# Half-size load buffers, doubled stage buffers and bf16 transposes in an eight-core attention-plus-masked-FFN kernel

## The reference

```python
xn = _layernorm(x, axis=-1)                       # x: (8, 2048, 2048), f32
# attention branch, 16 heads of 128, no softmax
q = relu(xn @ Wq) / SCALE; k = relu(xn @ Wk) / SCALE; v = xn @ Wv; u = silu(xn @ Wu)   # per head
kv = einsum('bhlk,bhlv->bhkv', k, v)
out = srms_norm(einsum('bhlk,bhkv->bhlv', q, kv)) * u
s = out @ Wo
# FFN branch: a router keeps 4 of 16 blocks for each token
mask = one_hot(top_k(softmax(xn @ Wr.T + br), 4))
h = gelu(einsum('nf,ibf->nib', xn, W1b)) * mask[:, :, None]     # W1b: 16 blocks of 512
g = silu(einsum('nib,fib->nf', h, W2b))
return x + s * g
```

## Time and profile before

| | |
|---|---|
| median of 2 runs | 6756.02 us (6677.65 to 6834.38) |
| the profiled execution | 6742.81 us, span 6741.0 us on core 3, the slowest |
| spans of the 8 cores | 6653.4 to 6741.0 us, mean granted TensorE clock 0.80 to 0.81 |
| busy share of the span | PE 54%, weight loads 22%, VectorE 19%, ScalarE 15%, GpSimd 6% |
| the chain that ended last | PE 50%, DMA 18%, VectorE 12%, ScalarE 9%, issue 8% |
| first transpose L209, last | 20.8 us, 657.0 us (stage 0) |
| first K matmul L308, last | 707.4 us, 1414.1 us (stage 1) |
| first W1 matmul L407, last W2 matmul L439 | 1428.1 us, 4487.3 us (stage 3) |
| first q matmul L510, last `bcp` matmul L564 | 4547.9 us, 6091.6 us (stage 2) |
| first output matmul L612, last | 6133.9 us, 6721.0 us (stage 4) |

### The profile page before, as it was taken

How to read it: one execution, slowest core, us unless ns; L and a number is a source line. 1 busy time by engine, 2 the same in 40 slices (tenths; PEclk the granted TensorE clock), 3 DMA queues, 4 the chain that set the end, 5 groups by cost and what they waited for, 6 DMA issues and landing times.

```text
span 6741.0 us, 45880 instructions; the slowest of 8 cores (6653.4 to 6741.0 us)
## 1 busy us (share of the span) xinstructions
PE 3666.1 (54%) x14994; PEld 1507.5 (22%) x14994; DVE 1300.4 (19%) x1958; ACT 985.9 (15%) x1317; POOL 378.5 (6%) x556
## 2 busy tenths in 40 slices
PE   2222777676666667656666766734444444444444
PEld 1111222232222223222222322311111111111111
DVE  2332000001222111112211111112223222321000
ACT  1111111111111111121111111111111111110000
POOL 0000000000000000000000000000000000002222
PEclk9999877898888888878888888866666666667777
DMA  1000111112222332322233232220000000003333
GB/s 39 25 26 22 47 50 50 44 59 86 89 89 90 94 100 81 100 75 88 88 94 100 81 100 83 86 81 13 25 25 19 19 25 25 13 25 78 93 90 89
DMA packets 130040, 422.73 MB, mean 63 GB/s; under 512 B 17104, under 2 KB 17104, under 8 KB 127760
## 3 DMA queue, kind: packets, MB, share of 16 engines
q1 hardware_dynamic: 83968, 251.76, 12.1%
q0 software_dynamic: 45840, 168.03, 8.3%
...
## 4 chain that ended last, share of the span: by engine, by line
PE 50%; DMA 18%; DVE 12%; ACT 9%; issue 8%; POOL 2%; DVEq 1%; ACTq 0%; POOLq 0%; SPq 0%
PE hps L407 15%; PE yps L439 14%; DMA w2ring<-w2t 7%; DMA gst<-gscr 4%; PE kp L308 4%; PE qp L510 4%; PE vp L313 4%; PE qp L519 3%; DVE srow L559 3%; ACT w1b L398 2%; ACT hm L411 2%; PE bcp L564 2%; PE pt L209 2%; DMA woring<-wo 2%; DVE w2b L428 2%
## 5 line engine op out<-in xcount | busy, mean ns | idle before, releaser
L439 PE MATMUL yps<-w2b,hm 128*128 128x512 bf16 x4096 | 946.4, 396 | 710.3 <-DVE w2b L428 710.3
L407 PE MATMUL hps<-A,w1b 128*128 128x512 bf16 x4096 | 1007.9, 409 | 317.0 <-ACT w1b L398 317.0
L439 PEld LDWEIGHTS yps<-w2b,hm 128*128 128x128 bf16 x4096 | 412.1, 101 | 1244.6 <-issue 802.0
L407 PEld LDWEIGHTS hps<-A,w1b 128*128 128x128 bf16 x4096 | 416.9, 104 | 908.8 <-issue 515.4
L612 PE MATMUL sps<-wob,osb 128*128 128x512 bf16 x1024 | 286.5, 445 | 342.2 <-ACT wob L598 198.6
L510 PE MATMUL qp<-A,wqb 128*128 128x512 bf16 x1024 | 255.2, 416 | 305.2 <-ACT wub L499 305.2
L447 DVE TENSOR_TENSOR y_acc<-y_acc,yps 128x1024 f32<-128x1024 f32 x224 | 273.6, 1222 | 597.5 <-PE yps L439 597.5
L564 PE MATMUL bcp<-srow,onesrfs 1*128 1x512 f32 x128 | 130.6, 1121 | 429.2 <-DVE srow L559 429.2
L308 PE MATMUL kp<-wkb,A 128*128 128x512 bf16 x1024 | 270.8, 425 | 146.0 <-ACT wvb L295 146.0
L415 DVE TENSOR_TENSOR hm<-hm,mbc 128x1024 bf16<-128x1024 bf16 x128 | 88.6, 692 | 1334.8 <-ACT hm L411 1334.8
L426 POOL DMA_DIRECT2D w2ring<-w2t x128 | 68.5, 535 | 3755.0 <-DVE w2b L428 3742.7
...
## 6 DMA issues: line engine op xcount, KB each, us to landing
w1ring<-w1r SPq DMA_DIRECT2D x256, 512.0 KB, 4.8
w2ring<-w2t SPq DMA_DIRECT2D x128, 512.0 KB, 5.4
w2ring<-w2t POOLq DMA_DIRECT2D x128, 512.0 KB, 4.4
...
wring<-wqr POOLq DMA_DIRECT2D x32, 512.0 KB, 4.8
wring<-wur POOLq DMA_DIRECT2D x32, 512.0 KB, 4.4
```

Source lines behind the costliest of these rows:

```text
L407: p.e("tensor", lambda e, i=i, ii=ii, ng=ng, sl=sl, hf=hf, tok0=tok0: e.matmul(hps[sl][:, ng * 512:(ng + 1) * 512], w1b[hf][:, ii * 128:(i ...
L439: p.e("tensor", lambda e, t8=t8, jc=jc, fg=fg, sl=sl: e.matmul(yps[sl][:, fg * 512:(fg + 1) * 512], hm[:, jc * 1024 + t8 * 128: jc * 1024 ...
```

## The change

Only the parts that the prediction speaks of; `...` marks what is left out. In stage 0 the split into high and low parts is made before the transposes, on the whole tile, and both parts are transposed as bf16. In stage 3 `w2b` gets two buffers (one for each fh), the W2 pieces are halved and cast by ScalarE, the mask rows come in halves through one buffer, and the silus work in place and are written out as f32. In stage 2 the body is split into `stage_qu(h)` and `stage_attn(h)`, called one head apart, with two buffers for `qtsb`, `utsb` and `attnsb`, half-size load pieces, and the squares done in two halves. In stage 4 `gst` is f32.

```diff
-    g_d = nc.dram_tensor("gscr", [L, D], BF16, kind="Internal").ap()
+    g_d = nc.dram_tensor("gscr", [L, D], F32, kind="Internal").ap()
...
+        xn_done = p.v(cV)
+        p.w("scalar", cV, xn_done)
+        p.e("scalar", lambda e: e.copy(out=xnhi[:], in_=xn32[:]), inc=cS)
+        hi_done = p.v(cS)
+        p.w("vector", cS, hi_done)
+        p.e("vector", lambda e: e.tensor_tensor(out=xnlo[:], in0=xn32[:], in1=xnhi[:], op=OP.subtract), inc=cV)
         ln_done[t] = p.v(cV)
...
-            p.e("tensor", lambda e, t=t, c=c, slot=slot: e.transpose(slot[:, 0:128], xn32[:, c * 128:(c + 1) * 128], idn32[:]), inc=cT)
+            p.e("tensor", lambda e, t=t, c=c, slot=slot: e.transpose(slot[:, 0:128], xnhi[:, c * 128:(c + 1) * 128], idnbf[:]))
+            p.e("tensor", lambda e, t=t, c=c, lslot=ptl[c % 2]: e.transpose(lslot[:, 0:128], xnlo[:, c * 128:(c + 1) * 128], idnbf[:]), inc=cT)
...
-            p.w("vector", cS, ahi_done[t][c])
             if c >= 2:
                 p.w("vector", cT, rt_done_c[c - 2])
-            p.e("vector", lambda e, t=t, c=c, slot=slot: e.tensor_tensor(out=alo[c % 2][:], in0=slot[:, 0:128], in1=A[:, c * L + t * 128: c * L + (t + 1) * 128], op=OP.subtract), inc=cV)
+            p.w("vector", cT, tr_done[t][c])
+            p.e("vector", lambda e, t=t, c=c, lslot=ptl[c % 2]: e.tensor_copy(alo[c % 2][:], lslot[:, 0:128]), inc=cV)
...
-    w2b = p3.enter_context(nc.sbuf_tensor("w2b", [128, 8 * 1024], BF16))
+    w2b = [p3.enter_context(nc.sbuf_tensor(f"w2b{i}", [128, 8 * 1024], BF16)) for i in range(2)]
-    w2ring = [p3.enter_context(nc.sbuf_tensor(f"w2ring{i}", [128, 1024], F32)) for i in range(2)]
+    w2ring = [p3.enter_context(nc.sbuf_tensor(f"w2ring{i}", [128, 512], F32)) for i in range(2)]
-    mrow = [p3.enter_context(nc.sbuf_tensor(f"mrow{i}", [1, 1024], BF16)) for i in range(2)]
+    mrow = p3.enter_context(nc.sbuf_tensor("mrow0", [1, 512], BF16))
...
                 for gg in range(2):
-                    p.e("tensor", lambda e, bb=bb, gg=gg: e.matmul(hps[0][:, gg * 512:(gg + 1) * 512], onesrb[0:1, :], mrow[bb][0:1, gg * 512:(gg + 1) * 512], start=True, stop=True), inc=(cT if gg == 1 else None))
+                    p.w("sync", cS, mask_done[NT - 1])
+                    p.w("sync", cT, mrow_guard[0])
+                    mrow_dma = p.dma("sync", lambda e, b=b, gg=gg, tok0=tok0: e.dma_start(out=mrow[0:1, :], in_=maskT[b:b + 1, tok0 + gg * 512: tok0 + (gg + 1) * 512]), dS)
+                    p.wd("tensor", mrow_dma)
+                    p.e("tensor", lambda e, gg=gg: e.matmul(hps[0][:, gg * 512:(gg + 1) * 512], onesrb[0:1, :], mrow[0:1, :], start=True, stop=True), inc=cT)
+                    mrow_guard[0] = p.v(cT)
...
-                    p.w(qeng, cV, w2cast_slot[sl])
-                    dd = p.dma(qeng, lambda e, jg=jg, fh=fh, sl=sl: e.dma_start(out=w2ring[sl][:], in_=w2t_d[jg * 128:(jg + 1) * 128, fh * 1024:(fh + 1) * 1024]), qsem)
-                    p.wd("vector", dd)
-                    p.e("vector", lambda e, jc=jc, sl=sl: e.tensor_copy(w2b[:, jc * 1024:(jc + 1) * 1024], w2ring[sl][:]), inc=cV)
-                    w2cast_slot[sl] = p.v(cV)
+                    for cc in range(2):
+                        p.w(qeng, cS, w2cast_slot[cc])
+                        dd = p.dma(qeng, lambda e, jg=jg, fh=fh, cc=cc: e.dma_start(out=w2ring[cc][:], in_=w2t_d[jg * 128:(jg + 1) * 128, fh * 1024 + cc * 512: fh * 1024 + (cc + 1) * 512]), qsem)
+                        p.wd("scalar", dd)
+                        if jc == 0 and cc == 0:
+                            p.w("scalar", cT, w2cons_fh[fh])
+                        p.e("scalar", lambda e, jc=jc, fh=fh, cc=cc: e.copy(out=w2b[fh][:, jc * 1024 + cc * 512: jc * 1024 + (cc + 1) * 512], in_=w2ring[cc][:]), inc=cS)
+                        w2cast_slot[cc] = p.v(cS)
...
-            p.wd("scalar", gst_dma[0])
-            p.e("scalar", lambda e, t8=t8: e.activation(out=gstage[:], in_=y_acc[:, t8 * D:(t8 + 1) * D], func=AF.Silu), inc=cS)
+            p.e("scalar", lambda e, t8=t8: e.activation(out=y_acc[:, t8 * D:(t8 + 1) * D], in_=y_acc[:, t8 * D:(t8 + 1) * D], func=AF.Silu), inc=cS)
...
-            for hf in range(2):
-                sslot = (h * 4 + (0 if wdst is wqb else 2) + hf) % 2
+            for hf in range(4):
+                sslot = hf % 2
...
-        qu_done = p.v(cS)
-        p.w("tensor", cS, qu_done)
+        qu_done[h] = p.v(cS)
+
+    def stage_attn(h):
+        par = h % 2
+        p.w("tensor", cS, qu_done[h])
...
-        p.e("vector", lambda e: e.tensor_tensor(out=sq32[:], in0=attnsb[:], in1=attnsb[:], op=OP.mult), inc=cV)
...
+        for hh2 in range(2):
+          p.e("vector", lambda e, par=par, hh2=hh2: e.tensor_tensor(out=sq32[:], in0=attnsb[par][:, hh2 * 1024:(hh2 + 1) * 1024], in1=attnsb[par][:, hh2 * 1024:(hh2 + 1) * 1024], op=OP.mult), inc=cV)
...
+    for h in range(NH):
+        stage_qu(h)
+        if h >= 1:
+            stage_attn(h - 1)
+    stage_attn(NH - 1)
...
-    gst = [p4.enter_context(nc.sbuf_tensor(f"gst{i}", [128, 512], BF16)) for i in range(2)]
+    gst = [p4.enter_context(nc.sbuf_tensor(f"gst{i}", [128, 512], F32)) for i in range(2)]
```

More of the change, by code:

```diff
@@ L138, in build @@
     nc.const_aps.register(F32, INV_SCALE, cst[:, 1:2])
-    for dst, src in ((idn32, idn32_d), (idnbf, idnbf_d), (onescol, onescol_d),
-                     (onesrb, onesrb_d), (onesrf, onesrf_d), (wrt32, wrr_d),
+    for dst, src in ((idnbf, idnbf_d), (onescol, onescol_d),
+                     (onesrb, onesrb_d), (onesrf, onesrf_d),
                      (br1, br_d), (cst, cst_d)):
         p.dma("gpsimd", lambda e, dst=dst, src=src: e.dma_start(out=dst[:], in_=src[:]), dG)
+    p0 = ExitStack()
+    wrt32 = p0.enter_context(nc.sbuf_tensor("wrt32", [128, NC * NB], F32))
+    p.dma("gpsimd", lambda e: e.dma_start(out=wrt32[:], in_=wrr_d[:]), dG)
     p.dbar("vector", dG)
@@ L163, in build @@
     maskb = p0.enter_context(nc.sbuf_tensor("maskb", [128, NB], BF16))
-    pt = [p0.enter_context(nc.psum_tensor(f"pt{i}", [128, 512], F32)) for i in range(2)]
+    pt = [p0.enter_context(nc.psum_tensor(f"pt{i}", [128, 128], BF16)) for i in range(2)]
+    ptl = [p0.enter_context(nc.psum_tensor(f"ptl{i}", [128, 128], BF16)) for i in range(2)]
     plog = p0.enter_context(nc.psum_tensor("plog", [128, 512], F32))
@@ L433, in build @@
+                w2_ready = p.v(cS)
+                p.w("tensor", cV, hm_ready)
+                p.w("tensor", cS, w2_ready)
                 for t8 in range(8):
                     sl = t8 % 2
-                    if t8 >= 2:
-                        p.w("tensor", cV, yadd[t8 - 2])
+                    p.w("tensor", cV, yadd_slot[sl])
                     for jc in range(8):
                         for fg in range(2):
-                            p.e("tensor", lambda e, t8=t8, jc=jc, fg=fg, sl=sl: e.matmul(yps[sl][:, fg * 512:(fg + 1) * 512], hm[:, jc * 1024 + t8 * 128: jc * 1024 + (t8 + 1) * 128], w2b[:, jc * 1024 + fg * 512: jc * 1024 + (fg + 1) * 512], start=(jc == 0), stop=(jc == 7)), inc=(cT if (jc == 7 and fg == 1) else None))
+                            p.e("tensor", lambda e, t8=t8, jc=jc, fg=fg, fh=fh, sl=sl: e.matmul(yps[sl][:, fg * 512:(fg + 1) * 512], hm[:, jc * 1024 + t8 * 128: jc * 1024 + (t8 + 1) * 128], w2b[fh][:, jc * 1024 + fg * 512: jc * 1024 + (fg + 1) * 512], start=(jc == 0), stop=(jc == 7)), inc=(cT if (jc == 7 and fg == 1) else None))
@@ L484, in build, with stage_qu @@
     o_done = {}
+    qu_done = {}
     wring2_slot = [0, 0]
-    for h in range(NH):
+    def stage_qu(h):
         par = h % 2
@@ L498, in build @@
                 first_cast = False
-                p.e("scalar", lambda e, par=par, hf=hf, sslot=sslot, wdst=wdst: e.copy(out=wdst[par][:, hf * 1024:(hf + 1) * 1024], in_=wring2[sslot][:]), inc=cS)
+                p.e("scalar", lambda e, par=par, hf=hf, sslot=sslot, wdst=wdst: e.copy(out=wdst[par][:, hf * 512:(hf + 1) * 512], in_=wring2[sslot][:]), inc=cS)
                 wring2_slot[sslot] = p.v(cS)
@@ L537, in build @@
             attn_evac[ng] = p.v(cV)
-        p.e("vector", lambda e: e.tensor_tensor(out=sq32[:], in0=attnsb[:], in1=attnsb[:], op=OP.mult), inc=cV)
-        sq_done = p.v(cV)
-        p.w("scalar", cV, sq_done)
-        p.e("scalar", lambda e: e.copy(out=sqh[:], in_=sq32[:]), inc=cS)
-        sqh_done = p.v(cS)
-        p.w("vector", cS, sqh_done)
-        p.e("vector", lambda e: e.tensor_tensor(out=sql[:], in0=sq32[:], in1=sqh[:], op=OP.subtract), inc=cV)
-        sql_done = p.v(cV)
-        p.w("tensor", cV, sql_done)
@@ L547, in build @@
-        for ng in range(4):
+        for hh2 in range(2):
+          p.e("vector", lambda e, par=par, hh2=hh2: e.tensor_tensor(out=sq32[:], in0=attnsb[par][:, hh2 * 1024:(hh2 + 1) * 1024], in1=attnsb[par][:, hh2 * 1024:(hh2 + 1) * 1024], op=OP.mult), inc=cV)
+          sq_done = p.v(cV)
+          p.w("scalar", cV, sq_done)
+          p.e("scalar", lambda e: e.copy(out=sqh[:], in_=sq32[:]), inc=cS)
```

(11 more changed lines are left out.)

81 lines of the change are left out of this document (39 added, 42 removed).

## The result

The changed kernel is slower: 1.032 times the time before (95% interval 1.022 to 1.042). The medians of all executions are 7032 us against 6876. Its profiled execution took 6831.29 us, span 6829.0 on core 6. The prediction said 6822 us and "within 2%", so the one number that it hit, the profiled time, hides that its start was wrong.

The account below looks back on a forecast made before the run. No single engine bounds the kernel; each stage is a chain of hand-overs between engines. Stage 0 -82, stage 3 +82, silus -36, stage 2 +89 and stage 4 +26 sum to +79 on 6742.8: 6822 us, range 6670 to 6935.

Parts of the forecast that it names:

- the gain of a chunk of stage 0: Stage 0, transposes and copies: each chunk saves 0.60 us (0.42 to 0.65), 256 chunks 154 us.
- the g piece: Stage 4, load of g doubled to 256 KB: 0.4 us more a tile, +26 us (0 to +45).
- from the last W2 matmul to the first W1 matmul: Stage 3, mask rows through one buffer delay the W1 loads: +7.0 us per slab (5 to 10).
- before fh 0: Stage 3, TensorE's wait for W2 loads and casts behind the last gelu: +10.7 us per slab.
- before fh 1: Stage 3, W2 loads and casts while TensorE does fh 0; wait 9.0 instead of 21.0, -12.0 us per slab.
- the silus: Stage 3, silus in place need 2.0 us each instead of standing 5.55 apart: -36 us (-50 to -10).
- short landings: Rival, faster: 256 KB pieces land 0.7 us sooner in stage 3 and the head loads; 6598 us, chance 0.07.
- longer hand-overs: Rival, slower: stage 3 mask-row DMAs take 2.8 us, SP rounds 4.7; slab +10.5, 6908 us, chance 0.20.
- (a): Stage 2, eight 256 KB loads a head instead of four of 512 KB: +4.75 us for 15 heads, +69 in all.
- (b): Stage 2, squares in halves: +2.1 us each, 16 x 2.1 = +34 us.
- (c): Stage 2, `ap` matmuls no longer wait for the last evacuation of u: about -0.9 x 16 = -14 us.
- the skew overlaps nothing: Stage 2, engines run in order, so the norm chain still stands alone, with no q, u matmuls beside it.

## Why the prediction was wrong, and where it was right

**In short.** Every step of the forecast happened in the direction that it said, and its sum still came to +79 us where the typical core lost 144. The terms that failed are sizes: the gain of a chunk of stage 0 (0.60 us said, 0.50 measured), the price of small pieces in a head (4.75 said, 5.8 measured), the g piece (0.4 said, 0.5 measured) and the time around the steps of stage 3 (9 us more). They failed all in one direction, and together they pass the 2% within which the forecast stayed.

**The base.** The sum was made against 6742.8 us, the slowest core of one execution, which had 60 us in stage 1 that the six typical cores did not have, at a granted clock of 0.79 there instead of 0.91. Its own table showed spans from 6653.4 to 6741.0, and the prediction did not use them. The typical core went from 6650.0 to 6794.3, +144 or 2.2%, where the sum said +79. That the profiled times differ by only 88.5 is chance, and so is it that 6822 lies near 6831. Of the measured 3.2%, the 2.2% are shown stage by stage. The 1.032 is what the mean of 6866.41, 6870.57 and 6937.36 us gives over that of 6670.45, 6677.65 and 6691.59. In the 6937.36 cores 2 and 3 stood 100 us above the six others at a granted clock of 0.78, the others at 0.79 to 0.80; without it the ratio would be 1.028. The rest of the last 1% lies in the slowest core's distance from the median core, which differs from execution to execution (72 us in the profile of before, 16 in that of after), and isn't resolved.

**Stage 0, forecast -82, measured -55.** The -59.5 of the table is counted from the first transpose, and the parts of the first tile now stand in front of it: it comes 4.3 us later (23.8 for 19.5, medians). The step from copy to subtraction went as said, the transposes take 0.37 as said, and the parts 4.5 us as said. What failed is the term of 0.60 a chunk: it was 0.50, and a tile takes 37.2 us instead of 40.7, where 35 was said. TensorE waits for both copies, which now end within 0.01 of each other (291.42 and 291.41), and it goes on 0.25 later, where it was 0.15 before. 256 x 0.10 = 26 us, and 27 are missing. What decides between 0.25 and 0.15 stays open. On core 7 it is 0.25 (median) in the 252 chunks in which ScalarE's copy ends last, and 0.15 in the four in which VectorE's does. That the two end together isn't the reason: the W2 matmuls after go on 0.25 after ScalarE's last cast (2399.45 against 2399.20), with VectorE done 30 us before. Behind ScalarE's W1 casts it is 0.14 in all 128 cases. A candidate that no run tests is the order of the waits in TensorE's list.

**Stage 3, forecast +46 with the silus, measured +52, and +3 in stage 1 for the first slab's mask rows.** Every step held, on core 7: from the last W2 matmul to the first W1 matmul +6.5 us (median 11.4 for 4.9) where +7.0 was said, before fh 0 +10.0 (mean 32.8 for 22.8) where +10.7 was said, before fh 1 -11.4 (10.5 for 21.9) where -12.0 was said. With these, a slab costs +5.1, as said. The silus stand 2.0 us apart; the change of halves is 23.6 us shorter without the mask rows' part (31.5 for 48.6, +6.5) and the end of the stage 10.3 (51.1 for 61.4), together -34 where -36 was said. The 9 us beyond the forecast lie in no single one of these steps. The size that decided the sign was the landing: 3.4 to 3.5 us for 256 KB here, as the earlier trace rows had it. By the Trainium skill, DMA: Bandwidth & Descriptors, section Anatomy of one DMA, whose fit is for the gpsimd path, it would be an estimated 2.6; the trace doesn't agree (3.5 on the POOL queue). The fixed part is the larger one in both: half the bytes took the POOL queue's landing from 4.4 to 3.5, so by that step 2.6 of the 3.5 don't shrink. The rivals of short landings and of longer hand-overs fall with it: 22.8 + 10.7 = 33.5 us was the forecast for the mean wait before fh 0, short landings would have made it 28, the slower hand-overs 36, and it is 32.8.

**Stage 2, forecast +89, measured +108.** (a) The loads cost 5.8 us a head instead of 4.75, 15 x 5.8 = 87 in all where 69 was said: before's price was read from the wait of head 1, 17.5, while the mean of 15 is 16.4. The total of that wait stood in the same view as the earlier trace rows. (b) Held, 2.4 for 2.1. (c) The sum of the stage leaves 108 - 87 - 38 = -17 for it, forecast -14. That the skew overlaps nothing held, and the experiment without it shows 1 us a head.

**Stage 4, forecast +26, measured +33.** That is 0.5 us a tile, where 0.4 was said. In the tiles in which VectorE waits for g it was 0.76, just above the upper bound of 0.7, but it doesn't wait in all 64.

**The chances.** All misses have the same sign: 27 + 9 + 19 + 7 are 62 of the 65 us between +79 and +144. A forecast at +79 with 2% at +135 left 0.27 for slower; a sum whose largest gain stood as near to its favourable bound as the 0.60 (0.42 to 0.65) should have had more.
